# Reordering the second sweep of a two-layer transformer kernel: key values before a norm's statistics, a dispatch matrix copied twice by ScalarE and split from SBUF, and silu before elu on VectorE

## The chip, the cores and the metric

The kernel runs on one NeuronCore of one Trainium2 chip. The time is the device time of one execution in microseconds (us); lower is better. TensorE (PE, with its weight loads as PEld), VectorE (DVE), ScalarE (ACT) and GpSimd (POOL) run their own instruction streams side by side and meet only at semaphores. SyncE (SP) issues the loads and stores. The matrix products write to PSUM, which here has eight banks of 128 x 512 f32; all else lies in SBUF.

## The reference

Sixteen sequences of 512 tokens with 128 features pass two layers. Layer 0 (a Mamba-like scan and an 8-expert feed-forward) fills the first sweep and is not touched. Layer 1 is what the second sweep computes:

```
h   = layernorm(x) * (1 + ca) + sa
# attention with softmax-kernel features, 16 heads of 64
qf  = exp(q @ proj - diag - max) + eps ; kf likewise
kv  = einsum('bnhm,bnhd->bhmd', kf, v)
attn = (qf @ kv) / (qf @ sum(kf))
out1 = layernorm(h + attn @ Wo) * g1 + b1n
o    = layernorm(out1 + elu(out1 @ W1 + b1) @ W2 + b2)
x   = x + ga * o
h   = layernorm(x) * (1 + cb) + sb
# mixture of 16 experts, the two best of each token, weighted by a softmax of their logits
moe = einsum('teh,te,edh->td', silu(h @ w1), dispatch, w2)
x   = x + gb * (moe + (silu(h @ sfc1) * (h @ sfc2)) @ sfc3)
```

## The kernel before, in words

The first sweep leaves each batch's normalized features (`h3`), residual (`x2`) and key sums (`kvl`) in DRAM. The second sweep goes over the 16 batches as a software pipeline. In step s each engine works on up to four batches in different roles: batch c = s in the attention, d = s - 1 in the feed-forward, e = s - 2 in the mixture of experts, and n = s + 1 for the key values. A step has 12 slots. Every engine's stream is written out slot by slot by its own `step(s)`, and nothing but this order and the semaphores decides what runs when.

In a slot below 8 the attention handles one half of 128 tokens x 8 heads: TensorE makes `q` (the query product) and `d` (its product with the projection), each a split product of three f32 matmuls of 512 columns (lines 174 to 176); ScalarE squares q (line 1543); VectorE's `exponent` reduces the squares and the maximum and subtracts (lines 1925 to 1931); ScalarE takes the exponential (line 1547). One slot later TensorE transposes the features (line 1741), two slots later `numerators` (line 1752) and VectorE's `quotient` follow, three slots later the quotient is transposed (line 1760), four slots later `output` (line 1768) adds the half to the attention result.

The feed-forward has four chunks. `feed_first` of chunk f (w0 to w3, a split product with `o1h` and `o1l`) is in slots 1 to 4. ScalarE's `elu` of the chunk does three activations in the same slot (lines 1581 to 1585), VectorE's `elu` makes `hE` (line 1972) one slot later, and TensorE's `feed_second` takes `hE` (line 1791) in that slot too, slots 2 to 5, behind `feed_first` of the next chunk where there is one.

The mixture has ten chunks q, in slots 1 to 10: TensorE makes `x` (`hidden`) and `y` (`factor`; from q = 2 on a product of `dT` with `pick`, line 1828), ScalarE `th` (line 1616), and VectorE's `silu` makes `sl` (line 2021), which reads the bank of x, and `hm` (line 2027), which reads the bank of y. `gates` in slot 0 ends with `disp`, the dispatch weights. `turn_dispatch` transposes them into a bank (line 1808), and they are kept as three bf16 parts in `dT`: ScalarE copies all three rows (`keep_dispatch`, line 1607), VectorE subtracts for the middle part and for the remainder `dR` (`split_dispatch`, lines 2008 and 2010), ScalarE rounds `dR` (`round_dispatch`, line 1611) and VectorE subtracts again (`low_dispatch`, line 2015).

PSUM banks are handed round. `orderC` and `orderD` list the uses of two rings of two banks each, with the signal that ends each use, and `freeC` and `freeD` make TensorE wait before a use for the last earlier use of the same bank. In ring D the uses of slots 1 and 2 before are x0, y0, w0, dT, x1, y1, w1: so w0 waits for sl0, dT for hm0, x1 for w0's `vb_ok`, y1 for dT's `d_rem`, w1 for sl1. In ring C the first query product of a batch (q0) takes the bank of the key values `kv0` and waits for `kvb_ok`.

At the end of a step VectorE does the statistics of the norm L5 behind the attention (lines 136 and 141), GpSimd makes `n_rs` from them (line 160), VectorE copies the key values of batch n (`keys`, lines 1943 and 1951) and then applies the norm to `n_xh` (line 149), which TensorE transposes in slot 0 of the next step, behind q0 (line 167).

Of the kernel before, what the change touches and what calls it, by code (L numbers as in the profile page):

```python
# [1293 lines left out]
def sweep_two(nc, ctx, sem, sig, sbuf, banks, pair, ident, iota, wv, pq_dram, modc, ones, half, mxrun, nmx, two, pickd,  # L1294
              gate_rows, x2_dram, h3_dram, kv_dram, out_v):
    with ExitStack() as part:
# [120 lines left out]
        for slot in range(SLOTS):  # L1417
            if slot < M:
                orderC += [(f"q{slot}", ATT, qsq, slot + 1), (f"d{slot}", ATT, qu, slot + 1)]
            if at_slot(slot, 1) is not None:  # L1420
                orderC += [(f"t{slot - 1}", ATT, qT_ok, slot)]
            if at_slot(slot, 3) is not None:
                orderC += [(f"a{slot - 3}", ATT, aT_ok, slot - 2)]
            if slot == HALVES:
                orderC += [("vs0", KEYS, evs_ok, 1), ("vs1", KEYS, evs_ok, 2)]
            if slot == HALVES + 1:
                orderC += [("kv0", KEYS, kvb_ok, 1), ("kv1", KEYS, kvb_ok, 1)]
            if slot == NORM7:
                orderD += [("turn7", FEED, L7.out, 1)]
            if slot in XQ:  # L1430
                q = XQ[slot]
                orderD += [(f"x{q}", MOE, sl_ok, q + 1), (f"y{q}", MOE, hm_ok, q + 1)]
            if slot in WF:
                orderD += [(f"w{WF[slot]}", FEED, vb_ok, WF[slot] + 1)]
            if slot == 1:
                orderD += [("dT", MOE, d_rem, 1)]

        def batch_at(s, off):

# [39 lines left out]
        with nc.Block() as block:  # L1479
# [47 lines left out]
            def _(act):  # L1527
# [76 lines left out]
                def keep_dispatch(e):  # L1604
                    act.wait_ge(*dtp(e, 1))
                    act.wait_ge(*yps(e, 0))
                    act.activation(dT[:, :], bankD("dT")[0:96, :], ACT.Copy).then_inc(dT_ok.sem, 1)

                def round_dispatch(d):
                    act.wait_ge(*d_rem(d, 1))  # L1610
# [8 lines left out]
                def step(s):  # L1619
                    c, d, e, n = roles(s)  # L1620
                    for slot in range(SLOTS):
                        if e is not None and slot == 2:
                            keep_dispatch(e)
                        if n is not None and slot == HALVES:
                            key_halves(n)
                        if c is not None and slot < M:
# [14 lines left out]
                            gates(e)  # L1641
                        if e is not None and slot == 2:
                            round_dispatch(e)
                        if c is not None and at_slot(slot, 3) is not None:
                            keep_quotient(at_slot(slot, 3), c)
                        if d is not None and slot in WF:
# [48 lines left out]
            def _(pe):  # L1695
# [148 lines left out]
                def step(s):  # L1844
                    c, d, e, n = roles(s)
                    for slot in range(SLOTS):
# [24 lines left out]
                            numerators(at_slot(slot, 2), c)  # L1871
                        if c is not None and at_slot(slot, 3) is not None:
                            turn_quotient(at_slot(slot, 3), c, s)
                        if d is not None:
                            if slot in WF:
                                feed_first(WF[slot], d, s)
                            if slot in WD:
                                feed_second(WD[slot], d, e)
                        if e is not None:
                            if slot == 1:  # L1880
                                turn_dispatch(e, s)
                            for q in DOWN.get(slot, ()):
                                down(q, e, d)
                        if n is not None:
# [8 lines left out]
            def _(dve):  # L1893
# [109 lines left out]

                def split_dispatch(d):

                    w = bankD("dT")
                    dve.wait_ge(*dT_ok(d, 1))
                    dve.tensor_tensor(dT[32:64, :], w[32:64, :], dT[32:64, :], ALU.subtract).then_inc(d_mid.sem, 1)
                    dve.wait_ge(*d_low(d, 0))
                    dve.tensor_tensor(dR[64:96, :], w[64:96, :], dT[64:96, :], ALU.subtract).then_inc(d_rem.sem, 1)  # L2010

                def low_dispatch(d):

# [16 lines left out]
                def step(s):  # L2030
# [1 line left out]
                    cC.begin(c)  # L2032
                    cD.begin(e)
                    for slot in range(SLOTS):
                        if e is not None and slot == 2:
                            split_dispatch(e)
                        if e is not None and slot == 3:
                            low_dispatch(e)
                        if n is not None and slot == HALVES:
# [7 lines left out]
                            low_half(o1l, o1T, o1h, o1_high, o1_low, d)  # L2047
                        if e is not None and slot == 0:
                            gates(e)
                        if d is not None:  # L2050
                            if slot == 6:
                                dve.wait_ge(*w2ps(d, 1))
# [6 lines left out]
                                low_half(h4l, hT4, h4h, h4_high, h4_low, d)  # L2059
                            if slot in WD:  # L2060
                                elu(WD[slot], d)
                        if e is not None and slot in XQ:
                            silu(XQ[slot], e)
                        if c is not None and at_slot(slot, 2) is not None:
                            quotient(at_slot(slot, 2), c)
                        if d is not None:
                            if slot == 8:
                                dve.wait_ge(*x3_ok(d, 1))
                                dve.wait_ge(*L7.turned(d, 0))
                                norm_stats(dve, L7, x2, d, passed)  # L2070
                            if slot == 9:
                                norm_apply(dve, L7, x2, d)
                    if c is not None:
                        dve.wait_ge(*wo_ok(c, M))
                        dve.wait_ge(*L5.turned(c, 0))
                        norm_stats(dve, L5, attn, c, passed)
                    if n is not None:
                        keys(n)
                    if c is not None:
                        norm_apply(dve, L5, attn, c)  # L2080
                    if e is not None:
                        dve.wait_ge(*mo(e, 1))
# [90 lines left out]
```

## Time and profile before

| what | value |
|---|---|
| median of 3 runs | 3527.33 us (3524.78 to 3529.87) |
| profiled execution | 3522.44 us |
| its span, first to last instruction | 3520.6 us |
| mean granted TensorE clock | 0.91 of 2.4 GHz |
| PE / DVE / ACT / POOL busy | 2912.7 / 2785.3 / 1985.7 / 899.6 us |
| the second sweep, from about 2113 us | about 1407 us |

The profile is one execution. An instruction's time is its start and duration on its engine; in square brackets stands how long its engine was idle just before, and whose result ended that. The row of a stretch gives its length, then the busy time and the number of instructions of PE, PEld, DVE, ACT and POOL in it, the granted clock of TensorE (1.00 is 2.4 GHz), and the share and GB/s of the DMA engines. All times are us from the start of the span unless marked ns. The second sweep's instructions carry the line numbers of the functions above, except for the helpers (lines 136 to 176), which are told apart by the names of their tiles.

### The profile page before, as it was taken

The numbers are of one execution on the slowest core, as the hardware profiler recorded it, in microseconds if no ns is written. First come the engines' busy times: TensorE is split into PE (matmuls) and PEld (weight loads), VectorE is DVE, ScalarE is ACT, GpSimd is POOL, SyncE is SP. The second block draws the span as 40 slices with busy tenths as digits, with TensorE's granted clock in tenths as the row PEclk, the third lists the DMA queues.
The fourth block names the chain that finished last, engine by engine and source line by source line (L and its number), as shares of the span: only waits on it lengthen the run. The fifth ranks groups of instructions, "written<-read, shape, count | busy, mean of one in ns | idle before, by whom it ended". The sixth has DMA issues, their size and how long they took to land. (4 is left out here: it accounts for less than half of the span.)

```text
span 3520.6 us, 53387 instructions
## 1 busy us (share of the span) xinstructions
PE 2912.7 (83%) x15912; PEld 2163.6 (61%) x15912; DVE 2785.3 (79%) x4750; ACT 1985.7 (56%) x4808; POOL 899.6 (26%) x607
## 2 busy tenths in 40 slices
PE   2377898898888888888898967898888888888887
PEld 1054565566556655655665735777777777777775
DVE  2999999999999999999999525676766676666664
ACT  3466677667676867776676533444444444444442
POOL 0443343433333333333333100111111111111110
PEclk6588999999999999999999988999999999999997
DMA  2000000000000000000000010000000000000000
GB/s 106 8 4 14 17 11 12 19 16 3 19 16 19 3 19 16 16 6 19 16 0 18 17 67 21 14 18 17 18 21 19 16 16 16 16 16 16 17 16 7
DMA packets 49779, 64.41 MB, mean 18 GB/s; under 512 B 3584, under 2 KB 36416, under 8 KB 49184
## 3 DMA queue, kind: packets, MB, share of 16 engines
q1 hardware_dynamic: 47392, 54.93, 4.9%
q10 hardware_dynamic: 2304, 8.46, 0.6%
q8 instruction: 41, 0.67, 0.1%
q14 instruction: 42, 0.34, 0.0%
HBM read 41.78 MB, written 21.60 MB: 18 GB/s over the span
## 5 line engine op out<-in xcount | busy, mean ns | idle before, releaser
L789 POOL TENSOR_TENSOR acc<-acc,zz 128x1024 f32<-128x1024 f32 x256 | 607.7, 2374 | 1010.3 <-DVE h L1104 953.4
L1104 DVE TENSOR_TENSOR_SCAN h<-dec,u 128x1024 f32<-128x1024 f32 x256 | 585.3, 2286 | 13.2 <-issue 4.8
L918 PEld LDWEIGHTS bank<-one_sb,hid 128*128 128x128 f32 x4096 | 483.4, 194 | 31.1 <-issue 17.2
L918 PE MATMUL bank<-one_sb,hid 128*128 128x128 f32 x4096 | 485.1, 277 | 14.6 <-ACT hid L654 14.6
L866 PE MATMUL bank<-S,pick_sb 96*128 96x512 bf16 x512 | 209.7, 414 | 249.6 <-DVE zz L1116 136.6
L158 POOL TENSOR_SCALAR n_ve<-n_mv 128x4 f32<-128x4 f32 x96 | 58.4, 609 | 1273.5 <-DVE n_mv L141 1273.5
L622 ACT ACTIVATE dec<-dt,aneg 128x512 f32<-128x512 f32 (+1 forms) x512 | 341.2, 722 | 63.4 <-DVE h L1104 47.6
L866 PEld LDWEIGHTS bank<-S,pick_sb 96*128 96x128 bf16 x512 | 50.1, 98 | 442.7 <-DVE zz L1116 199.8
L1116 DVE TENSOR_TENSOR zz<-h,bank 128x1024 f32<-128x1024 f32 x256 | 312.5, 1221 | 12.0 <-PE bank L866 2.0
L1097 DVE TENSOR_TENSOR u<-dtx,bank 128x1024 f32<-128x1024 f32 x256 | 309.7, 1210 | 0.4 <-PE bank L866 0.3
L654 ACT ACTIVATE hid<-banks,one_sb 128x512 f32<-128x512 f32 x304 | 208.1, 691 | 109.1 <-PE bank L918 65.6
L1616 ACT ACTIVATE th<-bank 128x512 f32<-128x512 f32 x160 | 95.3, 595 | 242.5 <-PE bank L176 242.3
L1925 DVE TENSOR_REDUCE qs<-qsqb 128x8 f32<-128x512 f32 x128 | 87.4, 683 | 144.4 <-ACT qsqb L1543 144.0
L2021 DVE SCALAR_TENSOR_TENSOR sl<-th,bank 128x512 f32<-128x512 f32 x160 | 108.7, 679 | 113.3 <-ACT th L1616 113.2
L1547 ACT ACTIVATE uq<-uq 128x512 f32<-128x512 f32 x128 | 80.7, 631 | 181.2 <-DVE uq L1931 181.2
L1543 ACT ACTIVATE qsqb<-bank 128x512 f32<-128x512 f32 x128 | 75.6, 590 | 187.6 <-PE bank L176 187.6
L654 ACT ACTIVATE hid<-bank,one_sb 128x512 f32<-128x512 f32 x208 | 145.6, 700 | 62.6 <-PE bank L918 53.6
L678 ACT ACTIVATE Gs<-banks 128x64 f32<-128x64 f32 x768 | 160.7, 264 | 22.4 <-PE banks L940 21.2
L1839 PE MATMUL bank<-two_sb,hm 128*128 128x128 f32 x1280 | 158.9, 278 | 7.8 <-DVE n_xh L149 7.8
L1839 PEld LDWEIGHTS bank<-two_sb,hm 128*128 128x128 f32 x1280 | 151.4, 194 | 11.7 <-DVE n_xh L149 11.5
L678 ACT ACTIVATION_READ_ACCUMULATOR Gs<-banks 128x1 f32 x768 | 158.5, 251 | 0.0
L174 PE MATMUL banks<-hT2h,w_low 128*128 128x512 f32 x304 | 153.7, 505 | 5.0 <-ACT hid L654 3.9
(269 smaller groups left out, 7136.5 us busy)
## 6 DMA issues: line engine op xcount, KB each, us to landing
kv_dram<-Gs ACTq DMA_DIRECT2D x16, 516.5 KB, 3.1
kvl<-kv_dram SPq DMA_DIRECT2D x16, 516.5 KB, 3.5
xs<-in_x SPq DMA_DIRECT2D x16, 256.0 KB, 2.8
x<-in_x SPq DMA_DIRECT2D x16, 256.0 KB, 3.0
x_dram<-x SPq DMA_DIRECT2D x16, 256.0 KB, 2.1
h_dram<-hT SPq DMA_DIRECT2D x16, 256.0 KB, 2.0
h<-h_dram SPq DMA_DIRECT2D x16, 256.0 KB, 2.6
x2s<-x_dram SPq DMA_DIRECT2D x16, 256.0 KB, 3.6
```

Source lines behind the costliest of these rows:

```text
L174: pe.matmul(dst, lhs[1], rhs[0], start=True, stop=False)
L622: act.activation(dec[:, k % 2, g, g:], dt[:, g, g:], ACT.Exp, scale=aneg[:, g, k:k + 1]).then_inc(dec_ok.sem, 1)
L654: act.activation(hid[:, e % 2, f, :], bank1(f"up{n}"), ACT.Relu, bias=b1c[:, n:n + 1]).then_inc(hid_ok.sem, 1)
L678: last = act.activation(sq[:, m % 2, head * DH:(head + 1) * DH], bank1(f"k{m}")[:, head * DH:(head + 1) * DH], ACT.Square, accum_out=ssq[: ...
L789: pool.tensor_tensor(acc[:, :, :], acc[:, :, :], zz[:, k % 2, :, :], ALU.add)\
L866: pe.matmul(banks[which][:, :], pick_sb[:, at:at + 1].to_broadcast([96, P]), S[0:96, :], start=True, stop=True).then_inc((cbc if which els ...
L918: last = pe.matmul(bank1(f"down{e}")[:, j * D:(j + 1) * D], hid[:, e % 2, f, j * P:(j + 1) * P], w2[:, e, f, :], start=(f == 0), stop=(f = ...
L1097: dve.tensor_tensor(u[:, :, :], dtx[:, :, :], mid(banks[0][:, :], G), ALU.mult)\
L1104: dve.tensor_tensor_scan(h[:, :, :].rearrange("p g t -> p (g t)"), dec[:, k % 2, :, :].rearrange("p g t -> p (g t)"), u[:, :, :].rearrange ...
L1116: dve.tensor_tensor(zz[:, k % 2, :, :], h[:, :, :], mid(banks[1][:, :], G), ALU.mult)\
L1839: last = pe.matmul(banks[7][:, j * D:(j + 1) * D], hm[:, q, j * P:(j + 1) * P], w, start=(q == 0 and j == 0), stop=(q == NX - 1), skip_gro ...
L2021: dve.scalar_tensor_tensor(sl[:, q % 2, :], th[:, q % 2, :], 1.0, bankD(f"x{q}")[:, :], ALU.add, ALU.mult).then_inc(sl_ok.sem, 1)
```

## The change

Three orders are changed, and the dispatch's copy.

1. VectorE copies the key values of batch n before the statistics of the attention norm, not between statistics and application.
2. TensorE transposes the dispatch ahead of w0 in slot 1, so ring D now runs x0, y0, dT, w0, x1, y1, w1: dT waits for sl0, w0 for hm0, x1 for dT, y1 for w0. ScalarE's `keep_dispatch` moves from the start of slot 2 to slot 1, ahead of elu of chunk 0, waits also for the last batch's `d_low`, and copies the bank twice, as bf16 into `dT` and as f32 into `dR`. The bank is free after that. VectorE's `split_dispatch` reads `dR` in SBUF instead of the bank, and moves from the start of slot 2 to behind the exponent and the silu of slot 2.
3. In slots 2 to 5 VectorE does `silu` (sl, hm) before `elu` (hE), not after.

```diff
--- before.py
+++ after.py
@@ -1430,10 +1430,10 @@
             if slot in XQ:
                 q = XQ[slot]
                 orderD += [(f"x{q}", MOE, sl_ok, q + 1), (f"y{q}", MOE, hm_ok, q + 1)]
+            if slot == 1:
+                orderD += [("dT", MOE, dT_ok, 1)]
             if slot in WF:
                 orderD += [(f"w{WF[slot]}", FEED, vb_ok, WF[slot] + 1)]
-            if slot == 1:
-                orderD += [("dT", MOE, d_rem, 1)]
 
         def batch_at(s, off):
 
@@ -1604,7 +1604,9 @@
                 def keep_dispatch(e):
                     act.wait_ge(*dtp(e, 1))
                     act.wait_ge(*yps(e, 0))
-                    act.activation(dT[:, :], bankD("dT")[0:96, :], ACT.Copy).then_inc(dT_ok.sem, 1)
+                    act.wait_ge(*d_low(e, 0))
+                    act.activation(dT[:, :], bankD("dT")[0:96, :], ACT.Copy)
+                    act.activation(dR[:, :], bankD("dT")[0:96, :], ACT.Copy).then_inc(dT_ok.sem, 1)
 
                 def round_dispatch(d):
                     act.wait_ge(*d_rem(d, 1))
@@ -1619,8 +1621,6 @@
                 def step(s):
                     c, d, e, n = roles(s)
                     for slot in range(SLOTS):
-                        if e is not None and slot == 2:
-                            keep_dispatch(e)
                         if n is not None and slot == HALVES:
                             key_halves(n)
                         if c is not None and slot < M:
@@ -1641,6 +1641,8 @@
                             gates(e)
                         if e is not None and slot == 2:
                             round_dispatch(e)
+                        if e is not None and slot == 1:
+                            keep_dispatch(e)
                         if c is not None and at_slot(slot, 3) is not None:
                             keep_quotient(at_slot(slot, 3), c)
                         if d is not None and slot in WF:
@@ -1871,14 +1873,14 @@
                             numerators(at_slot(slot, 2), c)
                         if c is not None and at_slot(slot, 3) is not None:
                             turn_quotient(at_slot(slot, 3), c, s)
+                        if e is not None and slot == 1:
+                            turn_dispatch(e, s)
                         if d is not None:
                             if slot in WF:
                                 feed_first(WF[slot], d, s)
                             if slot in WD:
                                 feed_second(WD[slot], d, e)
                         if e is not None:
-                            if slot == 1:
-                                turn_dispatch(e, s)
                             for q in DOWN.get(slot, ()):
                                 down(q, e, d)
                         if n is not None:
@@ -2003,11 +2005,9 @@
 
                 def split_dispatch(d):
 
-                    w = bankD("dT")
                     dve.wait_ge(*dT_ok(d, 1))
-                    dve.tensor_tensor(dT[32:64, :], w[32:64, :], dT[32:64, :], ALU.subtract).then_inc(d_mid.sem, 1)
-                    dve.wait_ge(*d_low(d, 0))
-                    dve.tensor_tensor(dR[64:96, :], w[64:96, :], dT[64:96, :], ALU.subtract).then_inc(d_rem.sem, 1)
+                    dve.tensor_tensor(dT[32:64, :], dR[32:64, :], dT[32:64, :], ALU.subtract).then_inc(d_mid.sem, 1)
+                    dve.tensor_tensor(dR[64:96, :], dR[64:96, :], dT[64:96, :], ALU.subtract).then_inc(d_rem.sem, 1)
 
                 def low_dispatch(d):
 
@@ -2032,8 +2032,6 @@
                     cC.begin(c)
                     cD.begin(e)
                     for slot in range(SLOTS):
-                        if e is not None and slot == 2:
-                            split_dispatch(e)
                         if e is not None and slot == 3:
                             low_dispatch(e)
                         if n is not None and slot == HALVES:
@@ -2047,6 +2045,10 @@
                             low_half(o1l, o1T, o1h, o1_high, o1_low, d)
                         if e is not None and slot == 0:
                             gates(e)
+                        if e is not None and slot in XQ:
+                            silu(XQ[slot], e)
+                        if e is not None and slot == 2:
+                            split_dispatch(e)
                         if d is not None:
                             if slot == 6:
                                 dve.wait_ge(*w2ps(d, 1))
@@ -2059,8 +2061,6 @@
                                 low_half(h4l, hT4, h4h, h4_high, h4_low, d)
                             if slot in WD:
                                 elu(WD[slot], d)
-                        if e is not None and slot in XQ:
-                            silu(XQ[slot], e)
                         if c is not None and at_slot(slot, 2) is not None:
                             quotient(at_slot(slot, 2), c)
                         if d is not None:
@@ -2070,13 +2070,12 @@
                                 norm_stats(dve, L7, x2, d, passed)
                             if slot == 9:
                                 norm_apply(dve, L7, x2, d)
+                    if n is not None:
+                        keys(n)
                     if c is not None:
                         dve.wait_ge(*wo_ok(c, M))
                         dve.wait_ge(*L5.turned(c, 0))
                         norm_stats(dve, L5, attn, c, passed)
-                    if n is not None:
-                        keys(n)
-                    if c is not None:
                         norm_apply(dve, L5, attn, c)
                     if e is not None:
                         dve.wait_ge(*mo(e, 1))
```

## Rows read from the trace of the kernel before

**Rows 1.** The page, part 1: busy us (share of the span), instructions.
```profile
PE 2912.7 (83%) x15912; PEld 2163.6 (61%) x15912; DVE 2785.3 (79%) x4750; ACT 1985.7 (56%) x4808; POOL 899.6 (26%) x607
```

**Rows 2.** Waits, second sweep: who for whom, us in total, times, longest.
```profile
PE bank L174 <- DVE sl L2021: 77.2, 48, 3.8
...
DVE dT L2008 <- ACT dT L1607: 49.9, 16, 3.5
...
PE bank L174 <- DVE kvb L1951: 37.7, 16, 4.0
```

**Rows 3.** Timeline, end of one step: start us, us, instruction, idle before.
```profile
2742.62 1.95 PE L1726 MATMUL bank<-keep_sb,kvl 128*128 128x128 f32 x16
...
2745.50 0.89 DVE L136 BATCH_NORM_STATS2 n_st<-bank 128x6 f32<-128x128 f32 x4 [2.56 <-PE bank L1768]
...
2747.32 1.98 DVE L1951 SCALAR_TENSOR_TENSOR kvb<-bank,sfac,evs 64x256 f32<-64x256 f32 x4
2747.47 1.02 POOL L160 TENSOR_TENSOR n_rs<-n_ve,half 128x4 f32<-128x4 f32 x1
2749.34 1.37 DVE L149 TENSOR_SCALAR n_xh<-bank,n_mv,n_rs 128x128 f32<-128x128 f32 x4
...
2749.45 0.47 PE L174 MATMUL bank<-high,h3l 128*128 128x512 f32 x1 [2.20 <-DVE kvb L1951]
...
2750.85 0.63 PE L167 MATMUL bank<-keep_sb,n_xh 128*128 128x128 f32 x4 [0.47 <-DVE n_xh L149]
```

**Rows 4.** Timeline, slots 1 and 2 of the next step, three engines.
```profile
2763.40 0.68 DVE L2021 SCALAR_TENSOR_TENSOR sl<-th,bank 128x512 f32<-128x512 f32 x1
...
2764.13 0.50 PE L174 MATMUL bank<-o1h,low 128*128 128x512 f32 x1 [3.82 <-DVE sl L2021]
...
2764.94 0.99 PE L1808 MATMUL bank<-keep_sb,disp 128*96 128x128 f32 x4
2765.14 0.69 ACT L1581 ACTIVATE vb<-bank,two_sb 128x512 f32<-128x512 f32 x1 [0.51 <-PE bank L176]
...
2766.97 0.58 ACT L1607 ACTIVATE dT<-bank 96x512 bf16<-96x512 f32 x1
...
2767.58 0.68 DVE L2008 TENSOR_TENSOR dT<-bank,dT 32x512 bf16<-32x512 f32 x1 [2.78 <-ACT dT L1607]
...
2769.01 0.69 DVE L1925 TENSOR_REDUCE qs<-qsqb 128x8 f32<-128x512 f32 x1
...
2771.26 0.68 DVE L1972 SCALAR_TENSOR_TENSOR hE<-ee,vb 128x512 f32<-128x512 f32 x1
...
2771.86 0.68 DVE L2021 SCALAR_TENSOR_TENSOR sl<-th,bank 128x512 f32<-128x512 f32 x1
...
2772.60 0.51 PE L174 MATMUL bank<-o1h,low 128*128 128x512 f32 x1 [1.36 <-DVE sl L2021]
...
2775.81 1.91 PE L1791 MATMUL bank<-two_sb,hE 128*128 128x128 f32 x8
```

**Rows 5.** Timeline, slots 4 and 5 of that step, TensorE and VectorE.
```profile
2790.10 0.51 PE L174 MATMUL bank<-o1h,low 128*128 128x512 f32 x1 [0.22 <-DVE sl L2021]
...
2795.81 0.68 DVE L1972 SCALAR_TENSOR_TENSOR hE<-ee,vb 128x512 f32<-128x512 f32 x1
...
2796.76 1.06 PE L1791 MATMUL bank<-two_sb,hE 128*128 128x128 f32 x8
...
2797.13 0.69 DVE L2027 SCALAR_TENSOR_TENSOR hm<-sl,bank 128x512 f32<-128x512 f32 x1
```

**Rows 6.** Stretches: three from w1 to w3, one whole step; length, busy us, clock, DMA.
```profile
2603.20:2622.18 18.98, 18.76 (x100) 15.44 (x100) 10.44 (x20) 9.43 (x17) 0.00 (x0) 0.82 0.00 0
...
2772.60:2790.10 17.50, 17.28 (x101) 14.56 (x101) 10.44 (x20) 9.52 (x17) 0.00 (x0) 0.90 0.00 0
2857.69:2873.58 15.89, 15.67 (x100) 13.05 (x101) 10.44 (x20) 9.55 (x17) 0.00 (x0) 1.00 0.00 0
...
2749.45:2834.37 84.92, 75.26 (x466) 64.03 (x467) 58.45 (x145) 36.94 (x65) 10.55 (x13) 0.92 0.06 17
```

## The prediction

> **What bounds the kernel now.** I read four views. First the page: over the whole span TensorE is 83% busy and VectorE 79% [rows 1]. That is an average over two sweeps with different limits, and the change touches only the second, which begins at about 2113 us. Then the stretches: one step of it, from one batch's first query product to the next one's, takes 84.92 us, with TensorE busy for 75.26 and VectorE for 58.45, at a granted clock of 0.92 [rows 6]. So TensorE nearly sets the pace, and what can be won is its 9.7 us of idle time per step and the time at a low clock. Then the waits of the sweep [rows 2]: TensorE stands 37.7 us in 16 waits behind `kvb` (the key values), 77.2 us behind `sl` (the first half of a silu), and VectorE 49.9 us in 16 waits behind the dispatch copy `dT`. Last the timeline of one step, to see what is late next once each wait goes. There are 14 full steps (with a batch in each of the roles c, d and e). The key values are copied 16 times, but the first time ahead of everything else, so they move in 15.
>
> **Part 1, key values ahead of the norm's statistics.** The eight key-value products run from 2742.62 to 2744.57, and VectorE has been idle for 2.56 us when it starts the statistics at 2745.50 [rows 3]. The copies (1.98 us in two halves) could start at about 2743.7, in that idle time, and end, the second half after 2744.57, at about 2745.6. TensorE's wait of 2.20 us for them then goes: q0 can start at 2747.25, as soon as TensorE is free. But what stands behind q0 is the transpose of the norm (line 167), and that needs `n_xh`. GpSimd's `n_rs` ends at 2748.49 [rows 3], and will end some 0.1 later, since the statistics start 0.1 later. VectorE applied the norm at 2749.34, after the copies; now it can at 2748.7. So of 2.20 + 0.47 us of waits only **0.6 us** comes back per step; the rest becomes a wait of line 167 of about 2 us. What follows it (logits, d0, the maximum of half 0, the gates) moves by that 0.6. 15 x 0.6 = **9 us**. Bounds: 0.3, if the statistics come 0.4 late, to the whole 2.67, which the `n_rs` row excludes; I keep 0.3 to 0.65.
>
> **Part 2, dispatch before w0, split after the exponent.** Count from the end of sl0, 2764.08, which moves with part 1 but with nothing else. Before, up to the start of w1 [rows 4]: w0 at 2764.13; ScalarE's three elu operations 1.01 later (2765.14); they take 1.83 to the copy of dT (2766.97); 0.61 to the first subtraction (2767.58, after VectorE idled 2.78 us); 1.43 for two subtractions; 2.85 from the exponent's first reduction (2769.01) to sl1 (2771.86), with 0.60 of it hE; 0.74 to w1 at 2772.60. That is 8.47 us behind w0's start.
> After: the four transposes of the dispatch take w0's place at 2764.13. w0 now waits for hm0, which follows sl0 on VectorE: 0.7 us later, at about 2764.85, while the transposes fill the gap. ScalarE copies twice meanwhile (0.6 us each at most, from about 2764.9 on), to about 2766.0, when w0 is also there: elu 0.15 us late at most, from 2766.0 to 2767.85. Now the square of half 2 comes next, not the dT copy. One ScalarE result to VectorE costs 0.61 (as above), so the exponent starts at 2768.45; 2.85 less hE's 0.60 leads to sl1 at 2770.7, and w1 starts at 2771.44. Gain 1.16, say **1.2 us**; 14 x 1.2 = **16.8 us**. Bounds: 0.9, if the second copy costs ScalarE's queue 0.3 more, to 1.9, the wait of 1.36 at w1 and half a microsecond of x1 and y1 now that y1 no longer waits for dR.
> The split lies on nobody's path any more: hm1 and two subtractions (0.72 + 1.43) and hE0 (0.65) end 2.75 us after w1's start, and TensorE asks for hE0 at 2775.81, 3.2 us behind it [rows 4]. Cover 0.45 us; if it is gone, the rest is lost. The new wait on ScalarE, rounding dR, holds elu of chunk 1 until about 2.6 us after w1's start, and with its 1.83 us ScalarE is free at 4.4; the next square needs hE0's products (1.91 us) and q3 and is due at about 5. Cover 0.6. The third new wait (the copies for last batch's `d_low`) was met a step ago.
> The subtractions now read SBUF alone. The nearest row for both forms: line 2015 does so already and takes 0.68 us, as lines 2008 and 2010 do from PSUM (that of line 2008 is shown [rows 4]); I cost this at nothing. The Trainium skill, page "VectorE: DVE Perf Modes", section on the TRN2 errata, charges a PSUM source 120 cycles and an SBUF source 58; an estimate from it is 0.065 us less for each subtraction, some 2 us over the sweep, and the trace's equal durations speak against it.
>
> **Part 3, elu's VectorE part behind silu.** In slots 2 to 4 it lets sl go 0.6 earlier, and w3 then no longer waits its 0.22 us [rows 5]. The price: hE and sl take 1.32 us from start to start (2795.81 to 2797.13), sl and hm as long, so hE comes 1.32 later. In slots 3 and 4 a feed-first product stands ahead of hE's user, and covers it to within 0.1 us. In slot 5 none does: hE3 ended at about 2796.49 and line 1791 started at 2796.76 [rows 5]; now it ends at 2797.81 and TensorE stands for 1.1 us. Less up to 0.2 for the earlier w3 (ScalarE's square of half 5 stands behind its elu), plus 0.05 of slot 3: **0.95 us lost**, 14 times: **13.3 us**. TensorE is busy without a pause before and after it, so nothing behind absorbs this. Bounds 0.85 to 1.15.
>
> **Part 4, the clock.** From w1 to w3 a step takes 15.85 to 15.90 us in ten of the 14 full steps, at a granted clock of 1.00; 17.50 at 0.90 in two, 18.98 at 0.82 in two [rows 6]. In these four TensorE, at 2.4 GHz else, fell to 1.2 GHz after the waits of w0 and w1, at a cost of 1.6 or 3.1 us each, 9.4 together. With the second wait (1.36 in the row shown) gone, I take two thirds: **6 us**; bounds 0 to 9.4.
>
> **Sum.** -9 - 16.8 + 13.3 - 6 = -18.5 us against the profiled execution's 3522.44 (span 3520.6, 1.8 outside it), 3503.9. The median of the runs is 4.9 us above that execution, so 3508.8: **3509 us**, 0.5% less.
>
> **Rivals.**
> *More of the clock comes back.* All falls between w1 and w3 vanish, part 1 gives 0.65, part 2 1.9 and elu costs 0.85: -9.8 - 26.6 + 11.9 - 9.4 = -33.9 us, and 3493. Ahead of that, q0 now runs before the first wait rather than after it; if this keeps d0 at the high clock, and d0 gives a third of the 1.6 us of a short fall [rows 6] in each step, 7 us more make it 3486. For it: ten steps of 14 are undisturbed behind w1 even now. Against: the waits ahead of w0 and line 167 are as long as before. Chance 0.18.
> *Elu takes it all back.* Part 1 gives 0.3, part 2 gives 0.9, elu costs 1.15 and the clock gives nothing: -4.5 - 12.6 + 16.1 = -1 us, 3526, no change that could be told. For it: three terms rest on covers of 0.1 to 0.45 us. Against: all must go one way. Chance 0.2.
> *Slower, by a clock fall in slot 5.* The new wait of about 1 us at line 1791 comes where TensorE runs densely. If it is followed by a fall as w1's is, each costs 1.6 to 3.1 us, in up to 14 steps: 22 to 43 us, so between 3531 and 3552. It outweighs the sum of the other parts from 18.5 us on, six falls of 3.1; for slower by over 0.2% it takes nine. For it: 1.4 us of waiting was followed by a fall in four steps. Against: that stage had a longer wait and thin work around it, and ten steps did not fall. Chance 0.12. The Trainium skill, page "TensorE: Matmul & The Clock Gate", section "HAM oscillation", describes this pattern: bursts of products that a wait separates each begin at the low clock. The stretches above agree for the long waits, and no row here shows it for one of 1 us alone.
>
> **How the numbers follow.** Forecast (3498 to 3519) 0.5. The measurement tells a change of about 0.2%, 7 us, from none. Faster by more: 0.5 + 0.18 and a little of the second rival, 0.69; within it 0.19; slower 0.12. The range takes in the first rival, with a little below it, the second, and the last up to a fall in six steps: 3482 to 3530.
>
> **What would show it.** Right: no wait of line 174 for `kvb`, but one of line 167 for `n_xh` of about 2 us; no VectorE wait for dT; w1 7.3 us behind the transposes; w1 to w3 at 15.9 in nearly all steps; a new wait at line 1791 of 1 us in slot 5; a step of about 83.5 us. Wrong: if line 1791 does not wait, I have undervalued the change by 13 us; if w1 still waits over 1 us for sl, part 2 failed; if the clock in slots 5 to 7 falls below 1.00, the last rival holds.

## The result and the profile after

The changed kernel takes 3532.53 us (median of 20 runs, 3526.57 to 3540.59), the kernel before 3524.87 us (20 runs, 3518.35 to 3533.76). The ratio is 1.0024, 95% interval 1.0016 to 1.0032: slower by a quarter of a percent, where the prediction had 0.5% faster. The forecast of 3509 us is off by 23.5 us, and the sign is wrong. The two profiled executions lie further apart (3522.44 and 3538.13 us, 15.7) than the medians (7.7), so what follows is read from stretches that repeat, not from the totals of the profiles.

The page of the changed kernel, span and part 1, against [rows 1], shows that no engine's busy time moves by more than the 15 us of ScalarE, whose second copy is new. What changed is when things run.

```profile
span 3536.3 us, 53414 instructions
...
PE 2911.9 (82%) x15912; PEld 2156.3 (61%) x15912; DVE 2788.4 (79%) x4750; ACT 2000.3 (57%) x4824; POOL 899.9 (25%) x607
```

The waits of its second sweep, against [rows 2]; lines between ScalarE's `keep_dispatch` and VectorE's `split_dispatch` have moved by one or two (1791 is now 1793, 1808 is 1810, 1839 is 1841):

```profile
PE bank L1810 <- DVE sl L2021: 52.7, 16, 4.0
PE bank L167 <- DVE n_xh L149: 40.6, 17, 3.4
...
PE bank L1841 <- DVE n_xh L149: 28.0, 15, 3.0
...
PE bank L1793 <- DVE hE L1974: 20.2, 31, 2.5
...
PE bank L174 <- DVE sl L2021: 11.0, 16, 1.2
...
PE bank L174 <- DVE kvb L1953: 3.3, 3, 1.7
```

The reader should see three things. The waits that the change aimed at are gone or small: `kvb` fell from 37.7 to 3.3, VectorE's wait for the dispatch copy (49.9) is gone, and w1 waits 5.6 us for `sl` in the 14 full steps instead of 20.8. The larger part of the waits for `sl`, ahead of the first product behind sl0, stays (52.7, now at line 1810). In the place of the first stands a wait of line 167, as forecast. And there are two new ones: line 1793 for hE, which was forecast, and line 1841, the first down product, for `n_xh` of norm L6: 28.0 us in 15 waits, which was not.

The timeline at the end of a step, against [rows 3]:

```profile
2749.39 1.95 PE L1728 MATMUL bank<-keep_sb,kvl 128*128 128x128 f32 x16
...
2750.49 1.98 DVE L1953 SCALAR_TENSOR_TENSOR kvb<-bank,sfac,evs 64x256 f32<-64x256 f32 x4 [0.39 <-PE bank L1728]
...
2752.49 0.89 DVE L136 BATCH_NORM_STATS2 n_st<-bank 128x6 f32<-128x128 f32 x4
...
2753.78 0.47 PE L174 MATMUL bank<-high,h3l 128*128 128x512 f32 x1
...
2755.49 1.37 DVE L149 TENSOR_SCALAR n_xh<-bank,n_mv,n_rs 128x128 f32<-128x128 f32 x4 [1.57 <-POOL n_rs L160]
...
2757.00 0.63 PE L167 MATMUL bank<-keep_sb,n_xh 128*128 128x128 f32 x4 [2.29 <-DVE n_xh L149]
```

The copies run in VectorE's idle time and end 0.02 us before the statistics; q0 no longer waits, and line 167 does for 2.29 us.

Slots 1 and 2, against [rows 4]:

```profile
2769.13 1.06 PE L1810 MATMUL bank<-keep_sb,disp 128*96 128x128 f32 x4 [3.99 <-DVE sl L2021]
...
2769.94 0.76 PE L174 MATMUL bank<-o1h,low 128*128 128x512 f32 x1
...
2770.22 0.59 ACT L1608 ACTIVATE dT<-bank 96x512 bf16<-96x512 f32 x1 [0.59 <-PE bank L1810]
...
2770.72 0.58 ACT L1609 ACTIVATE dR<-bank 96x512 f32<-96x512 f32 x1
...
2770.93 0.63 PE L176 MATMUL bank<-o1h,high 128*128 128x512 f32 x1
...
2771.60 0.69 ACT L1581 ACTIVATE vb<-bank,two_sb 128x512 f32<-128x512 f32 x1 [0.30 <-PE bank L176]
...
2776.90 0.51 PE L174 MATMUL bank<-o1h,low 128*128 128x512 f32 x1 [0.58 <-DVE sl L2021]
...
2777.60 0.68 DVE L2009 TENSOR_TENSOR dT<-dR,dT 32x512 bf16<-32x512 f32 x1
...
2779.03 0.69 DVE L1974 SCALAR_TENSOR_TENSOR hE<-ee,vb 128x512 f32<-128x512 f32 x1
...
2780.22 1.91 PE L1793 MATMUL bank<-two_sb,hE 128*128 128x128 f32 x8
```

w1 starts 7.77 us behind the transposes, against 8.47 behind w0 before; 7.3 was forecast. Half of the reason shows in w0's last product, which ran before like this:

```profile
2764.70 0.40 PE L176 MATMUL bank<-o1h,high 128*128 128x512 f32 x1
```

It takes 0.63 us now, at the low clock (granted 0.50 from 2769.94 to 2772.60), now that it stands behind the transposes. ScalarE's elu starts 1.66 us behind w0, not 1.01, and 2.47 behind the transposes, where 1.87 was forecast. The two copies are the other half: they end at 2771.30, 2.17 behind the transposes, so that elu would have been 0.3 late in any case. hE0 ends 0.50 us ahead of its user (0.45 was forecast), and the subtraction from SBUF takes 0.68 us as it did from PSUM.

Slots 5 to 7 of that step, against [rows 5] and beyond:

```profile
2800.34 0.68 DVE L2021 SCALAR_TENSOR_TENSOR sl<-th,bank 128x512 f32<-128x512 f32 x1
...
2801.66 0.68 DVE L1974 SCALAR_TENSOR_TENSOR hE<-ee,vb 128x512 f32<-128x512 f32 x1
...
2802.39 1.16 PE L1793 MATMUL bank<-two_sb,hE 128*128 128x128 f32 x8 [0.94 <-DVE hE L1974]
...
2810.67 1.04 POOL L160 TENSOR_TENSOR n_rs<-n_ve,half 128x4 f32<-128x4 f32 x1
...
2812.41 0.69 DVE L1933 TENSOR_TENSOR uq<-bank,nb 128x512 f32<-128x512 f32 x1
2813.01 0.68 DVE L2021 SCALAR_TENSOR_TENSOR sl<-th,bank 128x512 f32<-128x512 f32 x1
...
2813.73 0.69 DVE L2027 SCALAR_TENSOR_TENSOR hm<-sl,bank 128x512 f32<-128x512 f32 x1
2814.33 1.36 DVE L149 TENSOR_SCALAR n_xh<-bank,n_mv,n_rs 128x128 f32<-128x128 f32 x4
...
2815.74 2.05 PE L1841 MATMUL bank<-two_sb,hm 128*128 128x128 f32 x16 [1.79 <-DVE n_xh L149]
```

Here is the cause of the new wait of line 1841. In slot 7 `n_rs` is ready at 2811.71 and the exponent ends at 2813.10, but sl and hm stand ahead of the application of the norm. It starts at 2814.33 instead of 2813.01, 1.32 us later, and TensorE waits 1.79 us for it, where it waited 0.48 before.

Put side by side, the same step (starts on TensorE; the sum is q0 to the next q0):

| stretch | before | after | difference |
|---|---|---|---|
| q0 to the norm's transposes (line 167) | 1.40 | 3.22 | +1.82 |
| to the first product behind sl0 | 13.28 | 12.13 | -1.15 |
| to w1 | 8.47 | 7.77 | -0.70 |
| to q3 | 4.78 | 4.88 | +0.10 |
| to w3 | 12.72 | 12.36 | -0.36 |
| to feed-second of slot 5 | 6.66 | 8.25 | +1.59 |
| to the first down product | 11.91 | 13.35 | +1.44 |
| to the next q0 | 25.70 | 23.28 | -2.42 |
| sum | 84.92 | 85.24 | +0.32 |

The stretches ahead of w3 vary with the clock from step to step; those from w3 on repeat within 0.2 us in the other full steps, the last one excepted. From the last batch's q0 to the end of the span it was 180.1 us (from 3340.48 to 3520.6) and is 191.5 (from 3344.78 to 3536.3).

Stretches of the changed kernel, against [rows 6]: two from w1 to w3, and the whole step of the table.

```profile
2776.90:2794.14 17.24, 17.18 (x101) 14.45 (x101) 12.13 (x22) 9.76 (x18) 0.00 (x0) 0.90 0.00 0
2861.97:2877.60 15.63, 15.59 (x101) 12.97 (x101) 12.12 (x22) 9.73 (x18) 0.00 (x0) 1.00 0.00 0
...
2753.78:2839.02 85.24, 73.93 (x470) 62.22 (x468) 58.70 (x147) 37.80 (x66) 10.53 (x13) 0.94 0.05 17
```

From w1 to w3 six of the 14 full steps look like the first stretch, eight like the second.

### The profile page after: what moved, and what is told of

The parts are those of the page before. It is cut to its first block and busy times, and to the rows that moved or that the text cites. A ratio compares the mean times of both kernels' runs of the same rounds, so it can differ in the third digit from the quotient of the medians.

```text
span 3536.3 us, 53414 instructions
## 1 busy us (share of the span) xinstructions
PE 2911.9 (82%) x15912; PEld 2156.3 (61%) x15912; DVE 2788.4 (79%) x4750; ACT 2000.3 (57%) x4824; POOL 899.9 (25%) x607
```

## The experiments

Each ran in five rounds with the kernel before on the same chip, whose medians were 3522 to 3525 us; in each row the difference is to that one.

| kernel | median us | ratio, 95% interval | difference |
|---|---|---|---|
| changed kernel | 3532.53 | 1.0024 [1.0016, 1.0032] | +7.7 |
| 1, norm L6 first again | 3511.64 | 0.9960 [0.9947, 0.9973] | -12.0 |
| 2, elu first again too | 3487.30 | 0.9893 [0.9875, 0.9910] | -36.4 |
| 3, key values alone | 3514.78 | 0.9972 [0.9962, 0.9982] | -8.9 |
| 4, dispatch alone | 3502.51 | 0.9935 [0.9922, 0.9947] | -21.1 |
| 5, silu alone | 3554.69 | 1.0092 [1.0075, 1.0108] | +32.4 |
| 6, silu ahead in slots 2 to 4 | 3495.90 | 0.9922 [0.9908, 0.9937] | -26.4 |
| 7, key products behind the output | 3462.46 | 0.9830 [0.9816, 0.9843] | -59.8 |
| 8, split ahead of silu | 3530.67 | 1.0009 [0.9995, 1.0024] | +8.4 |
| 9, elu first in the draining step | 3509.30 | 0.9955 [0.9938, 0.9972] | -16.1 |
| 10, statistics behind silu in slot 6 | 3522.30 | 0.9999 [0.9989, 1.0010] | -1.0 |

The medians are of 4 to 12 executions, that of the changed kernel of 20. Kernels 1 to 4 and 9 ran on one chip, 5 to 8 on a second and 10 on a third. Where the text sets two kernels side by side it takes their medians; by the column of differences, 6 comes out 10.0 us behind kernel 2 (for 8.6), 7 ahead of it by 23.4 (for 25), 8 behind it by 44.8 (for 43), and 9 ahead of kernel 1 by 4.1 (for 2.3).

**1. Norm L6 first again.** In VectorE's step of the changed kernel:

```diff
-                        if e is not None and slot in XQ:
+                        if e is not None and slot in XQ and slot <= 5:
                             silu(XQ[slot], e)
...
                             if slot in WD:
                                 elu(WD[slot], d)
+                        if e is not None and slot in XQ and slot > 5:
+                            silu(XQ[slot], e)
```

> The changed kernel, with silu ahead only in slots 2 to 5; in slots 6 and 7 VectorE does the statistics and the application of norm L6 before silu again. Theory (the lost gain is silu standing ahead of that norm, so that TensorE's first down product, line 1841, waits 1.79 us for n_xh instead of 0.48): the wait is back at 0.5 us, the stretch from line 1793 in slot 5 to the first down product falls from 13.34 to 11.91 us in 14 full steps, and the kernel is 20 us faster than the changed one, about 6 us (0.2%) faster than before. Rival (that wait is only where a delay from slot 5 surfaces, or the clock is what costs): the wait of 1.0 us moves to another place, and the time stays within 5 us of the changed kernel.

Its timeline in slot 7:

```profile
2715.69 0.69 DVE L1933 TENSOR_TENSOR uq<-bank,nb 128x512 f32<-128x512 f32 x1
2716.30 1.36 DVE L149 TENSOR_SCALAR n_xh<-bank,n_mv,n_rs 128x128 f32<-128x128 f32 x4
...
2717.58 0.68 DVE L2021 SCALAR_TENSOR_TENSOR sl<-th,bank 128x512 f32<-128x512 f32 x1
2717.71 2.05 PE L1841 MATMUL bank<-two_sb,hm 128*128 128x128 f32 x16 [0.47 <-DVE n_xh L149]
```

The application follows the exponent at once, the wait is 0.47, the stretch from slot 5's feed-second to the first down product 12.0 us in every full step, and the kernel is 20 us faster than the changed one. The theory holds; the wait did not move elsewhere.

**2. Elu first again too.** The same edit with `slot <= 2` for `slot <= 5`: parts 1 and 2 without part 3.

> Parts 1 and 2 of the change with part 3 undone: silu is ahead of elu in slot 2 alone (where the split follows it); in slots 3 to 7 elu and norm L6 come first as before. Theory: no wait at the feed-second product of slot 5 and 0.5 us at the first down product; per full step 0.6 us from the key values and 1.2 from the dispatch remain, so 25 us (0.7%) faster than before. Rival (the clock takes it: six of 14 steps fell after w1 in the changed kernel, as four did before): 10 us or less faster than before.

36 us faster than before, where 25 were expected. Between 1 and 2 lie 24.3 us, the whole price of elu behind silu in slots 3 to 5. Its waits:

```profile
PE bank L167 <- DVE n_xh L149: 40.7, 17, 3.4
...
PE bank L174 <- DVE sl L2021: 14.3, 29, 1.5
...
PE bank L1841 <- DVE n_xh L149: 7.8, 15, 1.2
...
PE bank L1793 <- DVE hE L1974: 0.9, 1, 0.9
```

**3. The key values alone.**

```diff
+                    if n is not None:
+                        keys(n)
                     if c is not None:
                         dve.wait_ge(*wo_ok(c, M))
                         dve.wait_ge(*L5.turned(c, 0))
                         norm_stats(dve, L5, attn, c, passed)
-                    if n is not None:
-                        keys(n)
-                    if c is not None:
                         norm_apply(dve, L5, attn, c)
```

> The kernel before with the key values copied ahead of the statistics of L5 and nothing else. Theory: q0 starts 2.4 us earlier against the last down product, the logits 0.6 us earlier, 15 x 0.6 = 9 us or 0.25% faster than before. Rival (moving q0 ahead of the wait leaves a longer single wait ahead of thin work and costs clock): no change or slower.

8.9 us, as expected, and the mechanism holds: each full step has q0 to line 167 1.82 us longer and the stretch ahead of q0 2.44 shorter. That the median agrees to 0.1 us is partly luck. In the profile the kernel gains 3.6 us in the first filling step, where the sum had 0.6, loses 3.4 behind the last q0, and falls to the low clock behind w1 in six full steps instead of four.

**4. The dispatch alone.** Kernel 2 with the edit of 3 taken back.

> The kernel before with part 2 alone (dispatch transposed before w0, copied twice, split behind the exponent and the silu of slot 2, whose elu then comes last). Theory: from sl0 to w1 7.83 us instead of 8.5 to 9.2, so 14 x 1.2 = 16 us or 0.45% faster than before, and together with the kernel of the key values alone as much as parts 1 and 2 together. Rival (w1 earlier only moves the wait to the elu of chunk 1, held by the rounding of dR, or to lower clock): under 7 us.

21.1 us, for 16 expected. Together 3 and 4 give 30.0, and kernel 2, which has both, 36.4: the parts help each other by some 6 us, which no run here divides further. "Alone" is not quite true of it: silu is ahead of elu in slot 2 here as in all kernels with part 2, and experiment 5 shows what that does by itself.

**5. Silu alone.** The kernel before with silu in VectorE's step moved ahead of `if d is not None:`, in every slot.

> The kernel before with part 3 alone: VectorE does silu ahead of its whole feed-forward work in every slot (ahead of elu in slots 2 to 5, of norm L6 in slots 6 and 7). Theory: both costs seen in the changed kernel come back in full, 1.3 us behind w3 and 1.4 us behind slot 5 in each full step and some 7 us in the last two steps, about 45 us or 1.3% slower than before. Rival (the two costs depend on w1 being early): 20 us or less.

32.4 us slower, between theory and rival. Both stretches lengthen as in the changed kernel (w3 to slot 5's feed-second 8.28 us, on to the first down product 13.36), so the costs don't depend on w1 being early: in five of the full steps w1 came 8.5 to 8.6 us behind sl0, as late as in some steps of the kernel before, and the costs are the same in them. What the expectation left out is that here sl1 also gets ahead of hE0, and w1 comes 0.8 us earlier (mean from sl0 to w1 8.18, before 8.96): 11 us over 14 steps.

**6. Silu ahead in slots 2 to 4.** The edit of 1 with `slot <= 4`.

> Parts 1 and 2 with silu ahead of elu in slots 2, 3 and 4, and elu and norm L6 first from slot 5 on. Theory (only slot 5 has no feed-first product that covers hE): the wait of 0.22 us at w3 goes and one of up to 0.25 comes at hE2, so within 4 us of the kernel with elu first from slot 3 on. Rival (elu behind silu costs in each slot): a third of the 24 us per slot, so 16 us slower than that kernel.

8.6 us slower than kernel 2: not the 4 of the theory, not the 16 of the rival. TensorE waits 4.4 us in 17 waits for hE. In a full step w3 to slot 5's feed-second grows by 0.48 and q3 to w3 shrinks by 0.28, which makes 3 us; 3 more fall in the draining steps, and the rest is open. So the swap costs a little in slots 3 and 4 taken together and most in slot 5; only for slot 2 does a run (experiment 5) show a gain.

**7. Key products behind the output.** Kernel 4 with, on TensorE, the key products of slot 10 moved to slot 11:

```diff
                         if c is not None and at_slot(slot, 4) is not None:
                             output(at_slot(slot, 4), c)
+                        if n is not None and slot == SLOTS - 1:
+                            key_values(n, s)
...
-                            if slot == HALVES + 1:
-                                key_values(n, s)
```

> Part 2 alone plus another order for the key values: TensorE makes their products in slot 11 behind the last attention output instead of in slot 10 ahead of it; VectorE keeps statistics, key values, application. Theory (line 167 waits for n_xh, whose chain starts at the last output): the chain starts about 1.8 us earlier, the key values end with the down products, and line 167 starts 1.5 us earlier than in the kernel of parts 1 and 2, so about 20 us faster than that one, 3465 to 3470. Rival (the copies of the key values now end later, and q0 waits for them again): no faster than it.

```profile
2721.37 1.06 PE L1770 MATMUL bank<-two_sb,aT 128*128 128x128 f32 x8
2722.27 1.95 PE L1728 MATMUL bank<-keep_sb,kvl 128*128 128x128 f32 x16
2722.47 0.89 DVE L136 BATCH_NORM_STATS2 n_st<-bank 128x6 f32<-128x128 f32 x4 [0.77 <-PE bank L1770]
...
2724.29 1.98 DVE L1953 SCALAR_TENSOR_TENSOR kvb<-bank,sfac,evs 64x256 f32<-64x256 f32 x4
2724.44 1.02 POOL L160 TENSOR_TENSOR n_rs<-n_ve,half 128x4 f32<-128x4 f32 x1
2726.30 1.37 DVE L149 TENSOR_SCALAR n_xh<-bank,n_mv,n_rs 128x128 f32<-128x128 f32 x4
2726.41 0.47 PE L174 MATMUL bank<-high,h3l 128*128 128x512 f32 x1 [0.41 <-DVE kvb L1953]
...
2727.82 0.63 PE L167 MATMUL bank<-keep_sb,n_xh 128*128 128x128 f32 x4 [0.47 <-DVE n_xh L149]
```

The statistics now start as the key products start, the copies fill the time in which GpSimd makes `n_rs`, and waits of 0.41 and 0.47 us are left of 2.29. It is 25 us faster than kernel 2 and 1.7% faster than before: the best version here. Only 16.5 of the 25 are what the theory named: line 167 comes 1.2 us earlier behind the first down product in each of 14 steps (1.5 was expected). The other 8 lie between line 167 and the first product behind sl0, a stretch that takes 12.2 us in the mean at a granted clock of 0.89, against 12.8 at 0.79 in kernel 2; why the clock is higher there no run divides. The rival's wait for `kvb` is real (10.8 us in all), but small.

**8. Split ahead of silu.** Kernel 2 with `split_dispatch` and `silu` of slot 2 exchanged.

> Parts 1 and 2 with the split of the dispatch ahead of silu in slot 2, directly behind the exponent. Theory (of the 1.2 us won between sl0 and w1, most is that the split no longer stands ahead of sl1 on VectorE): w1 comes 1.4 us later, 14 x 1.4 = 20 us slower than the kernel of parts 1 and 2. Rival (the gain comes from ScalarE copying before elu and from the order of the banks): under 5 us slower.

43 us slower than kernel 2, twice the theory. Its stretches from w1 to w3, against [rows 6]; PEclk is the third number from the end:

```profile
2272.08:2291.20 19.12, 18.90 (x100) 15.37 (x100) 11.04 (x21) 8.99 (x16) 0.00 (x0) 0.82 0.00 1
2357.44:2376.53 19.09, 18.87 (x100) 15.37 (x100) 11.04 (x21) 8.99 (x16) 0.00 (x0) 0.82 0.01 1
...
2529.21:2545.10 15.89, 15.67 (x100) 13.06 (x100) 11.05 (x21) 8.99 (x16) 0.00 (x0) 1.00 0.00 0
2612.62:2630.07 17.45, 17.23 (x100) 14.50 (x100) 11.05 (x21) 8.98 (x16) 0.00 (x0) 0.90 0.00 0
```

w1 does come 1.5 us later (9.34 us behind sl0, for 7.85), which is 21 us. The other half lies in the clock: TensorE waits up to 2.1 us at w1, and in ten of the 14 full steps the stretch behind it then runs at 0.82 and takes 3.1 us more, in one at 0.90.

**9. Elu first in the draining step.** Kernel 1, with silu ahead in slots 3 to 5 only where `c is not None`.

> The kernel of the first experiment (silu ahead in slots 2 to 5, norm L6 first), but in the one step that has no attention batch any more, the last but one, elu comes first again from slot 3 on. Theory (of the 24 us that this order costs, 1.32 x 14 = 18.5 are the wait in slot 5 of full steps, and the rest falls in the draining step, where hE waits behind a silu that waits for its tanh): 3 to 5 us faster than that kernel, 3507 to 3509. Rival (the rest is clock): the same as that kernel within 2 us.

2.3 us less than kernel 1 by the medians, with overlapping intervals: inconclusive. In the profiles the time from the last q0 to the end is 181.8 us, in kernel 1 185.2, and the last feed-second product of the draining step waits 0.92 us for hE instead of 2.50. That agrees with the theory's 3 us but is one execution of each.

**10. Statistics behind silu in slot 6.** The edit of 1 with `slot <= 6`.

> The kernel of the first experiment, but silu ahead in slot 6 too: the statistics of L6 stand behind silu again, and only its application in slot 7 comes ahead of silu. Theory (GpSimd's n_rs is ready before the exponent of slot 7 ends, so only the silu ahead of the application delays n_xh): the wait at the first down product stays at 0.5 us, and the time within 3 us of that kernel, 3512. Rival (the late statistics are what delays n_xh): the wait is 1.8 us again and the kernel 20 us slower.

A miss in time, right in mechanism. The first down product's wait stays at 0.48 us and the stretch before it at 12.0, so it is the silu of slot 7 ahead of the application that cost 1.3 us per step, and the late statistics of slot 6 are covered in a full step. Yet the kernel is 10.7 us slower than kernel 1. In the profiles it takes 6.1 us more behind the last q0 (191.4 for 185.2): 1.6 of that is a clock fall behind w1 in the last full step, and some 4.4 lie in the draining steps, where the first down product waits 2.91 us for `n_xh`, a wait that experiment 1 doesn't have. Another 4.6 lie in the full steps before, in stretches in which both kernels have the same order (in all, seven of 14 steps fell behind w1, for five). Why the granted clock differs there stays open.

## Why the prediction was wrong

**The step that failed** is the first sentence of part 3, "In slots 2 to 4 it lets sl go 0.6 earlier", and all that it was built on: I read the moved `silu` as a swap with `elu`, in the slots that have one, and costed slot 5 as the only loss. The edit puts silu ahead of the whole `if d is not None:` block, in every slot, and not only "in slots 2 to 5", as the description of the change has it. In slots 6 and 7 this block holds the statistics and the application of norm L6, and the application has TensorE waiting behind it: 0.48 us even before. That row was in the list of waits of the kernel before (line 1839 for `n_xh`, 7.8 us in 15) and I didn't ask what the edit puts in front of it. With silu in front TensorE waits 1.79 us, and the stretch up to the first down product takes 13.34 us in every full step but the last, for 12.01 in experiment 1: 1.33 us, 18.6 in 14 steps, with some 3 more in the draining steps. By the medians, the changed kernel against experiment 1 shows 20 us.

The terms, in us, with what the runs put in their place:

| term | predicted | measured |
|---|---|---|
| part 1, key values | -9 | -8.9 (experiment 3) |
| part 2, dispatch | -16.8 | -21.1 (4) |
| parts 1 and 2 together | -25.8 | -36.4 (2) |
| part 3, elu in slots 3 to 5 | +13.3 | +24.3 (1 less 2) |
| part 3, norm L6 in slots 6 and 7 | not seen | +19.7 (changed kernel less 1) |
| part 4, clock behind w1 | -6 | 0 (six falls, 9.5 us, for four, 9.4; in the profiles) |
| sum | -18.5 | +7.7 |

*Part 1* was right in mechanism and size: line 167 took over the wait, 2.29 us for "about 2", and 2.42 less 1.82, 0.6 us, came back per step.

*Part 2* was right in mechanism, and its size was luck. In the changed kernel w1 comes 7.83 us behind sl0 in the median of the full steps, mean 7.80 for 8.96, so 1.16 us for the 1.2 predicted. But the prediction counted in one step, where it was 8.52 before, and expected about 7.36: in that kind of step only 0.7 us came back. Two errors cancel. The step it counted in is one of five in which w0's last product still ran at 0.40 us; in the other nine it ran at 0.63, elu started 1.6 to 1.7 us behind w0 instead of 1.0, and w1 came 9.1 to 9.2 us behind sl0. After the change w0 runs at 0.63 in all 14. The prediction had elu "0.15 us late at most"; it is 0.6 later than forecast. The time from sl0 to w1 is 7.8 us in 11 of the 14 steps now, where it was 8.5 or 9.2.

The rest of the 21 us of experiment 4 is not divided by any run. Its profile is 3.3 us shorter from the last q0 to the end (176.9 for 180.1), and its four falls behind w1 cost 6.4 us for 9.4. Nothing in the sum stood for the draining steps. The covers held: 0.50 us at hE0, and ScalarE, done with elu of chunk 1 at 2781.61, idles 1.64 us before the next square. The subtraction takes 0.68 us from SBUF as from PSUM; the estimate from the Trainium skill's page "VectorE: DVE Perf Modes", section on the TRN2 errata, of 0.065 us less is not borne out. Experiment 8 shows that moving the split off VectorE's path is what the part lives on: with the split ahead of silu w1 comes 9.34 us behind sl0, later than before the change (8.96). Of the gain, 0.60 us is hE0 moved behind sl1, as predicted; experiment 5, which moves nothing else there, has w1 0.60 earlier in each kind of step (8.60 for 9.20, 7.91 for 8.51).

*Part 3's* size was off even where its mechanism held. I took 0.2 us off for an earlier w3; w3 is 0.25 us earlier, but the product behind it then waits 0.25 for hE2 and comes 0.38 later behind w3, where the prediction had 0.05, and nothing is passed on. Slot 5 adds 1.21, so from w1 to slot 5's feed-second the step shown grows by 1.33 us, not 0.95: 18.6 us in 14 steps. Some 4.6 more fall in the draining steps (experiments 1 and 2 take 185.2 and 179.7 us from the last q0 on, of which 0.9 lies in the last full step), which again had no term.

*Part 4* failed. Falls between w1 and w3 were to vanish with w1's wait. The wait shrank to 0.58 us, and six of 14 steps fell, for four before; each by 1.6 us, so 9.5 in all for 9.4. It also looked at one stretch alone, and "at 2.4 GHz else" is not what the trace shows: from line 167 to the first product behind sl0 the granted clock was 0.74 in the mean of the 14 steps before, and is 0.80 after, in 12.61 us for 13.06. These 6 us, won where the first rival had looked for 7, stand in no term of the sum. Experiment 3, with part 1 alone, doesn't have them (13.03). The page "TensorE: Matmul & The Clock Gate" of the Trainium skill, section "HAM oscillation", was cited for the rival of a fall in slot 5: the changed kernel shows one, in the last full step, where a wait of 1.26 us at line 1793 was followed by a stretch at 0.89 that took 1.6 us longer; in the other 13, with 0.94 us, none. So that rival was not what made the kernel slower either. That each burst behind a wait begins at the low clock, as the prediction has it from there, these rows bear out only in part: after waits of 2.6 to 3.8 us w0's last product still ran at 0.40 us in five of the 14 steps before. The rival "elu takes it all back" had the right culprit but too little of it.

## What to carry to other kernels

When an instruction is moved ahead of a conditional block, list everything that the block holds in every iteration, and look up who waits for each; here the loss sat two slots away from the reason for the move. A consumer that already waits a little (0.48 us) for the last of a chain has no cover: whatever is put ahead of that chain costs in full. A sum counted in one step should be checked in the others first: here that step was one of five, and nine others were 0.6 to 0.7 us longer. And a pipeline's draining steps want a term of their own: orders that cost little or nothing in full steps cost 3 to 4.5 us in the last two (experiments 6 and 10).

## What the runs showed of the hardware

A short wait of TensorE can be followed by a fall of its clock that costs more than the wait. Behind w1 such a fall cost 1.6 us (granted 0.90 up to w3) or 3.1 us (0.82), and nothing in between was seen. Seven of the kernels and the changed one share the order of slot 1 in which w1 waits 0.6 us at most: in two to seven of their 14 full steps the clock fell (experiments 7 and 10 are the ends). All 35 falls are among the 44 steps in which w1 waited 0.56 to 0.59 us, and none is among the 68 with a shorter wait or none. With 0.8 to 1.7 us of waiting four steps fell in the kernel before and six in experiment 3, with 0.2 to 1.1 three in experiment 5, and with 1.2 to 2.1 us eleven in experiment 8.

These counts don't show that the wait causes the fall. Where w1 didn't wait, TensorE had been slower ahead of it (in experiment 2 a granted clock of 0.62 to 0.77 from the transposes to w1, and of 0.78 to 0.82 where it waited 0.55 us or more), so the wait and what went before it change together, and no run holds one of them still. Two kernels with the same order in those steps differed by 4.6 us in it.

A burst behind a long wait can start at the high clock and fall within it, and then it matters which product stands first. In the step shown the first product behind sl0 started after 3.82 us of waiting before and 3.99 after; w0's last product took 0.40 us where w0 came first and 0.63 us behind the transposes. It took 0.40 in five of the 14 full steps before, and in none after.
